# Met waits between the products of the output in 31 tiles of a fused Mamba and local-attention kernel

## The chip, the cores and the metric

The kernel runs on one core of one Trainium2 chip. The metric is device time in microseconds (us) of one execution. A core has a matrix engine (PE, which executes matmuls and, on a track called PEld, weight loads), a vector engine (DVE), an activation engine (ACT), a general engine (POOL) and an engine that issues DMAs (SP). Each has a sequencer of its own that walks through that engine's instructions in program order; engines meet only through semaphores, which count finished stages. A wait for a semaphore is an instruction of the waiting engine.

## The reference

The input is 4 sequences of 1024 tokens with 128 features, in float32. The reference normalises it, runs a bidirectional Mamba layer, and then six transformer layers. One transformer layer is, shortened:

```python
def attn_layer(x, Wqkv, qs, ksc, Wo):          # 16 heads of 64, window 32
    q, k, v = split(x @ Wqkv)                  # q, k: l2norm, scale, rotary
    out = local_attention(q, k, v)             # each window sees itself and the one before
    return out @ Wo
def ffn_layer(x, g, bln, W1, b1, W2, b2):
    a, gate = split(layernorm(x) * g + bln) @ W1 + b1
    return a * gelu(gate) @ W2 + b2
for i in range(6):
    x = attn_layer(shift_tokens(x), ...) + x
    x = ffn_layer(shift_tokens(x), ...) + x
```

The change touches `out @ Wo` of the attention, in the kernel a product of the mixed values with folded weights.

## The kernel before, in words

The Mamba layer fills the first 1,070 us or so. Then come the six layers, worked through in 192 tiles of 128 tokens (32 per layer, numbered 0 to 191 through all layers); four tiles are a chunk. For a tile PE does: `project0` and `project1` (L1043, queries and keys), four `head_turn` transposes (L1054), `score` (L1078 and L1093), `row_turn` (L1065), `mix` (L1105), `output` (L1116). Per chunk there are the feed-forward stages (L1141, L1154) and two means (L1123, L1129).

The order of these stages on PE is a table, `PE_ORDER`, one round per chunk, with stages of neighbouring chunks interleaved. The other engines have tables like it. So the work ahead of a tile's score or output depends on the tile's place in its chunk, its number modulo 4, and hardly on anything else; the text calls it place 0 to 3.

`after(engine, (stage, k))` (L900) puts in a wait until stage `k` is done. Several waits ahead of one matmul become separate wait instructions of PE, two waits in each, and the last wait rides on the matmul's weight load.

The number of an instruction in PE's program is counted as follows. A product of float32 operands is four instructions (two weight loads and two matmuls), a transpose or a product of rounded or bfloat16 operands two, a separate wait one. The score of a tile is 64 float32 products of 32 to 64 columns, 256 instructions, after two bfloat16 products (L1078). The trace shows each float32 product as two matmuls, so a score has 128 matmuls, and an output, 16 products, has 32. In this text "pair" means one weight load with its matmul; a score has 128 pairs.

Of the kernel before, what the change touches and what calls it, by code (L numbers as in the profile page):

```python
# [651 lines left out]
DEPTH, HEADS, HEAD_DIM, WINDOW = 6, 16, 64, 32  # L652
PAIRS = HEADS // 2
INNER = HEADS * HEAD_DIM
HIDDEN = int(DIM * 4 * 2 / 3)
HIDDEN_PARTS = [(0, P), (P, P), (2 * P, HIDDEN - 2 * P)]
QK_SCALE = 8.0
TILES = TOKENS // P
# [21 lines left out]
def head_at(place):  # L680

    return place % PAIRS * 2 + place // PAIRS
# [145 lines left out]
def transformer(nc, ctx, consts, xa, xb, resid, kept, kept_stored, hbm, out, stored):  # L828

    def sb(name, shape, dt=F32):  # L830
        return ctx.enter_context(nc.sbuf_tensor(name, shape, dt))
# [9 lines left out]
    w_vo = sb("w_vo", [P, 2, HEADS, P])  # L841
    w1_parts = sb("w1_parts", [P, 2, 2 * HIDDEN], F32R)
    w2 = sb("w2", [P, 2, 3, P])
# [29 lines left out]
    work = sb("work_ff", [P, BANK])  # L873
    hidden = [sb(f"hidden{k}", [m, BANK]) for k, (_, m) in enumerate(HIDDEN_PARTS)]
    ff_parts = sb("ff_parts", [P, 2, BANK], F32R)
# [5 lines left out]
    score_ps = ps[:, S:S + 2, :].rearrange("p b (h k) -> p (b h) k", k=2 * WINDOW)  # L881
    w1_raw = w_stage[:, 0:2 * HIDDEN]
    w_v, w_o = vo_stage[:, 0], vo_stage[:, 1]
# [16 lines left out]
    def after(eng, *producers):  # L900
        for name, k in producers:
            eng.wait_ge(done[name], k + 1)
# [6 lines left out]
    def indexed(name, f, n):  # L909
        return {f"{name}{i}": f(i) for i in range(n)}  # L910
# [12 lines left out]
    def place(tile):  # L923
        return tile // TILES, tile % TILES, tile % 2

    with nc.Block() as block:
# [63 lines left out]
        def _(pe):  # L990
# [11 lines left out]
            def turn_free(name, k, i=0):  # L1002
                last = TURNS[name, k, i][1]
                if last and last[0] == "ff_output":
                    ff_added(pe, CHUNKS + last[1])
                elif last and last[0] in ("fold0", "fold1"):
                    pe.wait_ge(vo_copied, 4 * last[1] + 2 * int(last[0] == "fold1") + last[2] + 1)
                elif last and last[0] == "mix":
                    after(pe, (f"copy_mixed{last[2]}", last[1]))
                elif last and last[0] == "in_variance":  # L1010
                    pe.wait_ge(done["in_rstd"], 2 * last[1] + 1)
                elif last:
                    after(pe, (TURN_READERS[last[0]], last[1]))
                return turn_bank(name, k, i)
# [94 lines left out]
            def output(tile):  # L1109
                l, t, odd = place(tile)  # L1110
                after(pe, *[(f"copy_mixed{w}", tile) for w in range(WINDOWS)])
                if t == 0:
                    pe.wait_ge(vo_copied, 4 * l + 4)
                bank = turn_free("output", tile)
                for place_h in range(HEADS):
                    last = pe.matmul(bank[:, 0:P], w_vo[:, l % 2, head_at(place_h), :], mixed[:, odd, place_h, :],  # L1116
                                     start=place_h == 0, stop=place_h == HEADS - 1)
                last.then_inc(done["output"], 1)

            def mean(chunk):  # L1120
# [10 lines left out]
            def hidden_part(name, first):  # L1131
                def part(k):
                    lo, m = HIDDEN_PARTS[k]

                    def stage(chunk):
                        after(pe, ("rest_high", chunk))
                        if chunk % CHUNKS == 0:
                            pe.wait_ge(w1_low, chunk // CHUNKS + 1)
                        bank = turn_free(f"{name}{k}", chunk)
                        for i, (wpart, xpart) in enumerate([(0, 0), (1, 0), (0, 1)]):  # L1140
                            last = pe.matmul(bank[0:m], w1_parts[:, wpart, first + lo:first + lo + m],  # L1141
                                             ff_parts[:, xpart, :], start=i == 0, stop=i == 2)
                        last.then_inc(done[f"{name}{k}"], 1)
                    return stage
                return part

            def ff_output(chunk):
# [4 lines left out]
                bank = turn_free("ff_output", chunk)  # L1152
                for k, (lo, m) in enumerate(HIDDEN_PARTS):
                    last = pe.matmul(bank, w2[0:m, l % 2, k, :], hidden[k][:, :], start=k == 0, stop=k == 2)  # L1154
                last.then_inc(done["ff_output"], 1)

            stages = {"in_centre": in_centre, "in_variance": in_variance, **indexed("fold", fold, 2), **indexed("project", project, 2), **indexed("head_turn", head_turn, 4),
                      "row_turn": row_turn, "score": score, "mix": mix,
                      "output": output, "mean": mean, "variance": variance,
                      **indexed("gate", hidden_part("gate", HIDDEN), 3), **indexed("value", hidden_part("value", 0), 3),  # L1160
                      "ff_output": ff_output}
# [4 lines left out]
        def _(act):  # L1166
# [120 lines left out]
            def gelu(k):  # L1287
                m = HIDDEN_PARTS[k][1]

                def stage(chunk):  # L1290
                    l = chunk // CHUNKS
                    if chunk % CHUNKS == 0:
                        act.wait_ge(w2_loaded, 32 * l + 32)
                    after(act, (f"gate{k}", chunk))
                    if chunk:
                        after(act, ("ff_output", chunk - 1))
                    act.activation(hidden[k][:, :], turn_bank(f"gate{k}", chunk)[0:m], ACT.Gelu,
                                   bias=lp[0:m, l % 2, GATE_B + k:GATE_B + k + 1]).then_inc(done[f"gelu{k}"], 1)
                return stage
# [26 lines left out]
        def _(dve):  # L1326
# [106 lines left out]
            def product(k):  # L1433
                m = HIDDEN_PARTS[k][1]

                def stage(chunk):
                    after(dve, (f"value{k}", chunk), (f"gelu{k}", chunk))
                    dve.scalar_tensor_tensor(out=hidden[k][:, :], in0=turn_bank(f"value{k}", chunk)[0:m],
                                             scalar=lp[0:m, chunk // CHUNKS % 2, A_B + k:A_B + k + 1],
                                             in1=hidden[k][:, :], op0=ALU.add, op1=ALU.mult).then_inc(done[f"product{k}"], 1)  # L1440
                return stage
# [188 lines left out]
def host_layout(inputs):  # L1630
# [11 lines left out]
    lp[:, :, LN_G], lp[:, :, LN_B], lp[:, :, OUT_B] = a["L0_ffn_ln_g"], a["L0_ffn_ln_b"], a["L0_ffn_b2"]  # L1642
    for k, (lo, m) in enumerate(HIDDEN_PARTS):
        w2[:, :m, k] = a["L0_ffn_W2"][:, lo:lo + m]
        lp[:, :m, A_B + k] = a["L0_ffn_b1"][:, lo:lo + m]
        lp[:, :m, GATE_B + k] = a["L0_ffn_b1"][:, HIDDEN + lo:HIDDEN + lo + m]
    return {
# [35 lines left out]
```

## Time and profile before

| | us |
|---|---|
| median of 2 runs | 3917.53 |
| the two runs | 3914.40, 3920.66 |
| span of the profiled execution, first to last instruction | 3921.5 |
| PE busy in that span | 3707.5 (95%) |
| POOL busy | 3241.5 (83%) |
| DVE busy | 3319.6 (85%) |
| ACT busy | 2915.4 (74%) |

A time of its own, beside its span, is not given for the profiled execution. Its span lies 4.0 us (0.1%) above the median of the runs. Busy shares of PE count a matmul until its modelled end, so successive matmuls overlap; the spacing of their starts is what a product costs. The rows that matter stand in a section below.

### The profile page before, as it was taken

The numbers are of one execution on the slowest core, as the hardware profiler recorded it, in microseconds if no ns is written. First come the engines' busy times: TensorE is split into PE (matmuls) and PEld (weight loads), VectorE is DVE, ScalarE is ACT, GpSimd is POOL, SyncE is SP. The second block draws the span as 40 slices with busy tenths as digits, with TensorE's granted clock in tenths as the row PEclk, the third lists the DMA queues.
The fourth block names the chain that finished last, engine by engine and source line by source line (L and its number), as shares of the span: only waits on it lengthen the run. The fifth ranks groups of instructions, "written<-read, shape, count | busy, mean of one in ns | idle before, by whom it ended". The sixth has DMA issues, their size and how long they took to land.

```text
span 3921.5 us, 110568 instructions
## 1 busy us (share of the span) xinstructions
PE 3707.5 (95%) x43392; PEld 2518.5 (64%) x43392; DVE 3319.6 (85%) x3407; ACT 2915.4 (74%) x6890; POOL 3241.5 (83%) x2370
## 2 busy tenths in 40 slices
PE   7889989988789999999999999999999999999997
PEld 2333333333377777777777777777767777777775
DVE  4999999999688888888888887888878888788885
ACT  7555445553388887888888887888878888888885
POOL 3888888888698888888888888888888888888883
PEclk8999998998899999999999999999999999999999
DMA  1221222212100000000000000000000000000001
GB/s 68 73 76 70 76 71 75 76 71 83 50 16 2 16 3 2 17 2 16 3 6 13 2 16 2 6 13 3 16 2 6 13 2 16 2 6 2 2 3 44
DMA packets 31567, 102.12 MB, mean 26 GB/s; under 512 B 4676, under 2 KB 6600, under 8 KB 30928
## 3 DMA queue, kind: packets, MB, share of 16 engines
q1 hardware_dynamic: 31056, 95.05, 7.0%
q8 instruction: 352, 5.77, 0.6%
q14 instruction: 159, 1.30, 0.1%
HBM read 90.32 MB, written 4.72 MB: 24 GB/s over the span
## 4 chain that ended last, share of the span: by engine, by line
PE 68%; issue 2%; ACT 2%; DVE 0%; POOL 0%; POOLq 0%; ACTq 0%; DVEq 0%
PE ps L1116 17%; PE ps L1043 13%; PE ps L1105 9%; PE ps L1054 8%; PE ps L1093 7%; PE ps L1141 5%; PE ps L1154 3%; PE ps L1078 2%; PE ps L1065 1%; PE ps L1123 1%; PE ps L1129 1%; ACT prob L1246 0%; PE ps L1023 0%; ACT mixed L1255 0%; ACT w_qk L1175 0%
## 5 line engine op out<-in xcount | busy, mean ns | idle before, releaser
L1521 POOL TENSOR_TENSOR resid<-resid,sq 128x1024 f32<-128x1024 f32 x384 | 910.8, 2377 | 3.4 <-DVE sq L1376 2.9
L626 POOL TENSOR_TENSOR read<-state,c_row 128x1024 f32<-128x1024 f32 x256 | 719.8, 2831 | 153.9 <-DVE state L588 84.9
L1543 POOL TENSOR_TENSOR resid<-resid,rnorm 128x1024 f32<-128x1024 f32 x384 | 725.0, 1904 | 18.1 <-POOL rnorm L1535 0.4
L1116 PE MATMUL ps<-mixed,w_vo 128*128 128x128 f32 x6144 | 720.7, 276 | 3.0 <-ACT mixed L1255 2.8
L1116 PEld LDWEIGHTS ps<-mixed,w_vo 128*128 128x128 f32 x6144 | 711.5, 193 | 12.9 <-issue 4.6
L1043 PE MATMUL ps<-w_qk,xs_parts 128*128 128x512 f32 x2304 | 634.6, 411 | 35.4 <-issue 18.1
L1246 ACT ACTIVATE prob<-ps,stat 128x64 f32<-128x64 f32 x3072 | 653.5, 385 | 0.7 <-DVE stat L1396 0.5
L1376 DVE TENSOR_TENSOR sq<-ps,rope_l 128x1024 f32<-128x1024 f32 x384 | 462.4, 1204 | 101.5 <-ACT sq L1208 101.2
L393 PE MATMUL mamba_ps<-read,ident 128*128 128x512 f32 x1024 | 509.6, 638 | 15.4 <-POOL read L626 15.4
L1389 DVE TENSOR_TENSOR resid<-ps,rope_l 128x1024 f32<-128x1024 f32 x384 | 464.3, 1209 | 66.9 <-ACT sq L1208 59.7
L1043 PEld LDWEIGHTS ps<-w_qk,xs_parts 128*128 128x128 f32 x2304 | 412.4, 191 | 148.6 <-issue 73.8
L1550 POOL TENSOR_TENSOR prob<-prob,stat 128x1024 f32<-128x1024 f32 x192 | 366.1, 1907 | 165.3 <-DVE stat L1407 165.3
L1208 ACT ACTIVATE sq<-ps 128x1024 f32<-128x1024 f32 x384 | 395.7, 1030 | 141.3 <-PE ps L1043 111.8
L1255 ACT COPY mixed<-ps 128x512 f32<-128x512 f32 x768 | 399.5, 602 | 111.8 <-PE ps L1105 111.7
L522 ACT ACTIVATE decay<-dt,neg_a 128x1024 f32<-128x1024 f32 x256 | 280.4, 1143 | 268.1 <-DVE state L588 212.6
L1353 DVE TENSOR_REDUCE ssq<-sq 128x16 f32<-128x1024 f32 x384 | 465.7, 1213 | 6.1 <-ACT sq L1208 1.7
L1054 PE MATMUL ps<-ident,resid 128*128 128x128 f32 x3072 | 414.4, 275 | 13.7 <-ACT w_vo L1190 13.1
L588 DVE TENSOR_TENSOR_SCAN state<-decay,mamba_ps 128x1024 f32<-128x1024 f32 x176 | 396.3, 2274 | 3.7
L1054 PEld LDWEIGHTS ps<-ident,resid 128*128 128x128 f32 x3072 | 351.3, 141 | 74.6 <-issue 60.8
L1105 PE MATMUL ps<-prob_t,rows 32*128 32x512 f32 x3072 | 385.2, 613 | 4.1 <-DVE xb L1424 1.6
L393 PEld LDWEIGHTS mamba_ps<-read,ident 128*128 128x128 f32 x1024 | 196.9, 202 | 283.5 <-issue 247.1
L1230 ACT COPY q_t<-ps 128x512 f32<-128x512 f32 x384 | 230.9, 602 | 127.0 <-PE ps L1054 125.0
(138 smaller groups left out, 5676.8 us busy)
## 6 DMA issues: line engine op xcount, KB each, us to landing
c_row<-c_rows SPq DMA_DIRECT2D x128, 512.0 KB, 3.6
w_stage<-w_qk_hbm SPq DMA_DIRECT2D x12, 512.0 KB, 4.7
vo_stage<-w_v_hbm SPq DMA_DIRECT2D x6, 512.0 KB, 3.7
vo_stage<-w_o_hbm SPq DMA_DIRECT2D x6, 512.0 KB, 4.6
xn<-x_hbm SPq DMA_DIRECT2D x4, 512.0 KB, 6.6
kept<-resid SPq DMA_DIRECT2D x8, 256.0 KB, 4.4
resid<-kept SPq DMA_DIRECT2D x8, 256.0 KB, 4.0
out_hbm<-resid SPq DMA_DIRECT2D x8, 256.0 KB, 2.0
```

The source lines that it names most:

```text
L393: last = pe.matmul(y_ps[h][:, c, :], ident[:, :], read[:, h, g % 2, cols(c)], start=False, stop=n == LAST)
L626: pool.tensor_tensor(read[:, h, g % 2, :], state[:, h, g % 2, :], c_row[:, g % C_AHEAD, :], ALU.mult).then_inc(done[f"rd{h}"], 1)
L1043: last = pe.matmul(ps[:, A + c, :], xs_parts[:, odd, xpart, :], w_qk[:, wpart, cols], start=k == 0, stop=k == 2)
L1054: last = pe.transpose(bank[:, j * P:(j + 1) * P], qk[:, tile % 2, col:col + P], ident[:, :])
L1105: last = pe.matmul(banks[w], rows[rows_w, tile % 2, own, :], prob_t[rows_w, tile % 2, :, own, :], start=own == 0, stop=own == 1)
L1116: last = pe.matmul(bank[:, 0:P], w_vo[:, l % 2, head_at(place_h), :], mixed[:, odd, place_h, :], start=place_h == 0, stop=place_h == HEADS ...
L1246: last = act.activation(prob[:, tile % 2, place_h, :], score_ps[:, place_h, :], ACT.Exp, bias=stat[:, tile % 2, 0, place_h:place_h + 1])
L1353: dve.tensor_reduce(ssq[:, tile % 2, part * HEADS:(part + 1) * HEADS, 0], sq[:, 0, :].rearrange("p (h d) -> p h d", d=HEAD_DIM), AX_X, ALU ...
L1376: dve.tensor_tensor(sq[:, 1 + part, :].rearrange("p (h s d) -> p h s d", s=2, d=HEAD_DIM // 2), swapped, table(part, 1, tile).rearrange("p ...
L1389: dve.tensor_tensor(qk[:, tile % 2, part * INNER:(part + 1) * INNER].rearrange("p (h d) -> p h d", d=HEAD_DIM), heads_ps.rearrange("p (h d ...
L1521: pool.tensor_tensor(qk[:, tile % 2, cols], qk[:, tile % 2, cols], sq[:, 1 + part, :], ALU.add).then_inc(done[f"rotated{part}"], 1)
L1543: pool.tensor_tensor(heads, heads, norms, ALU.mult).then_inc(done[f"normed{part}"], 1)
```

## The change

In 31 of the 192 tiles, waits for `copy_mixed0` of the same tile are put ahead of the products 2 to 16 of `output`. The first product has waited for that very stage already, so each of the new waits is met when PE's sequencer comes to it. A table gives the number of added wait instructions per tile, from 16 to 60; the code spreads them over the 15 places between the products, the larger shares first (60 is four at each place, 35 is three at five places and two at ten). Of the `2 * spaced` waits at a place the last rides on the next product's weight load, and the others make `spaced` separate wait instructions (two waits in each, one in the odd one). In all, 1,363 instructions are added to PE's program; the order of the work on every engine is the same, and so are all products.

```diff
+FETCH_PADS = {0: 35, 3: 35, 15: 58, 16: 58, 17: 34, 21: 34, 26: 41, 39: 60, 40: 60, 41: 28, 53: 60, 54: 55, 60: 60, 61: 42, 
+    73: 18, 85: 59, 86: 56, 92: 59, 93: 43, 105: 17, 117: 59, 118: 56, 124: 59, 125: 43, 137: 17, 149: 49, 
+    154: 39, 167: 16, 175: 60, 176: 16, 184: 37}
@@ output(tile)
                 for place_h in range(HEADS):
                     last = pe.matmul(bank[:, 0:P], w_vo[:, l % 2, head_at(place_h), :], mixed[:, odd, place_h, :],
                                      start=place_h == 0, stop=place_h == HEADS - 1)
+                    spaced = (FETCH_PADS.get(tile, 0) + HEADS - 2 - place_h) // (HEADS - 1) if place_h < HEADS - 1 else 0
+                    for _ in range(2 * spaced):
+                        after(pe, ("copy_mixed0", tile))
                 last.then_inc(done["output"], 1)
```

PE's program about the output of tile 60 (place 0; 60 added waits), with the semaphores that each matmul and the wait instructions ahead of it wait for; L1043 is a projection, L1129 a variance, L1065 the row turns, L1116 the output. Before:

```order
L1043 MATMUL ps<-w_qk,xs_parts 128x512 [waits sines1,cosines1,rest]
L1043 MATMUL ps<-w_qk,xs_parts 128x512 x5
L1129 MATMUL ps<-work_ff,ones_mean 128x512 [waits copy_mixed0,square]
L1065 MATMUL ps<-ident,xa 128x128 [waits copy_mixed1,x_ready,x_low]
L1116 MATMUL ps<-mixed,w_vo 128x128 [waits copy_mixed3,copy_mixed2,copy_mixed1,copy_mixed0]
L1116 MATMUL ps<-mixed,w_vo 128x128 x15
L1054 MATMUL ps<-ident,resid 128x128 [waits copy_mixed3,normed0]
```

And now (the lines below the table of pads have moved by three, those below the output by six):

```order
L1046 MATMUL ps<-w_qk,xs_parts 128x512 [waits sines1,cosines1,rest]
L1046 MATMUL ps<-w_qk,xs_parts 128x512 x5
L1135 MATMUL ps<-work_ff,ones_mean 128x512 [waits copy_mixed0,square]
L1068 MATMUL ps<-ident,xa 128x128 [waits copy_mixed1,x_ready,x_low]
L1119 MATMUL ps<-mixed,w_vo 128x128 [waits copy_mixed3,copy_mixed2,copy_mixed1,copy_mixed0]
L1119 MATMUL ps<-mixed,w_vo 128x128 [waits copy_mixed0] x15
L1057 MATMUL ps<-ident,resid 128x128 [waits copy_mixed3,normed0]
```

Nothing has changed places; 15 of the 16 products now have waits ahead of them (four instructions each here, which the row shows once).

The same about the output of tile 85 (place 1; 59 added waits), where L1141 is a gate product and L1054 a head turn. Before:

```order
L1054 MATMUL ps<-ident,resid 128x128 [waits copy_mixed3,normed1]
L1054 MATMUL ps<-ident,resid 128x128 x3
L1141 MATMUL ps<-ff_parts,w_parts 128x512 [waits copy_heads0,rest_high]
L1141 MATMUL ps<-ff_parts,w_parts 128x512 x2
L1116 MATMUL ps<-mixed,w_vo 128x128 [waits copy_mixed3,copy_mixed2,copy_rows,copy_mixed1,copy_mixed0]
L1116 MATMUL ps<-mixed,w_vo 128x128 x15
L1054 MATMUL ps<-ident,resid 128x128 [waits x_ready,x_low,normed1]
```

And now:

```order
L1057 MATMUL ps<-ident,resid 128x128 [waits copy_mixed3,normed1]
L1057 MATMUL ps<-ident,resid 128x128 x3
L1147 MATMUL ps<-ff_parts,w_parts 128x512 [waits copy_heads0,rest_high]
L1147 MATMUL ps<-ff_parts,w_parts 128x512 x2
L1119 MATMUL ps<-mixed,w_vo 128x128 [waits copy_mixed3,copy_mixed2,copy_rows,copy_mixed1,copy_mixed0]
L1119 MATMUL ps<-mixed,w_vo 128x128 [waits copy_mixed0] x15
L1057 MATMUL ps<-ident,resid 128x128 [waits x_ready,x_low,normed1]
```

Here too only the 15 later products have gained waits, and every instruction of PE behind them has a higher number in the program.

## Rows read from the trace of the kernel before

**Rows 1.** The page, part 1: busy us, share of the span, instructions of each engine.

```profile
PE 3707.5 (95%) x43392; PEld 2518.5 (64%) x43392; DVE 3319.6 (85%) x3407; ACT 2915.4 (74%) x6890; POOL 3241.5 (83%) x2370
```

**Rows 2.** Windows view, layers: us, busy us per engine (PE, PEld, DVE, ACT, POOL), clock, DMA.

```profile
1500.00:3850.00 2350.00, 2318.10 (x34556) 1791.23 (x34555) 1980.77 (x2321) 1970.49 (x5230) 2024.62 (x1723) 1.00 0.02 7
```

**Rows 3.** Waits of PE, 1500 to 3850 us: total us, times, longest.

```profile
PE ps L1043 <- issue: 14.4, 5, 3.6
PE ps L1093 <- issue: 2.7, 9, 0.5
```

**Rows 4.** The page, part 3: DMA queue, packets, MB, share of 16 engines.

```profile
q8 instruction: 352, 5.77, 0.6%
```

**Rows 5.** Source view of L902, PE's separate waits: duration ns min/median/max, first and last start.

```profile
L902 PEldq EVENT_SEMAPHORE  x3111: 51/51/3933, 1041.4 to 3911.3; - x195
```

**Rows 6.** Timeline of PE, scores of tiles 4, 33 and 185: start, us, matmuls, idle before.

```profile
1123.36 1.31 PE L1093 MATMUL ps<-k_t,q_t 64*32 64x64 f32 x109
1125.04 0.41 PE L1093 MATMUL ps<-k_t,q_t 64*32 64x64 f32 x19 [0.36 <-issue]
...
1551.47 1.48 PE L1093 MATMUL ps<-k_t,q_t 64*32 64x64 f32 x128
...
3781.47 1.47 PE L1093 MATMUL ps<-k_t,q_t 64*32 64x64 f32 x126
3783.39 0.27 PE L1093 MATMUL ps<-k_t,q_t 64*32 64x64 f32 x2 [0.46 <-issue]
```

**Rows 7.** DMA view, packets that started from 1122.3 to 1122.4 us: packets, MB, share.

```profile
q8 instruction: 1, 0.02, 77.5%
```

**Rows 8.** Timeline of PE, scores of tiles 96 and 124.

```profile
2479.51 1.46 PE L1093 MATMUL ps<-k_t,q_t 64*32 64x32 f32 x128
...
2883.38 1.20 PE L1093 MATMUL ps<-k_t,q_t 64*32 64x64 f32 x100
2884.91 0.45 PE L1093 MATMUL ps<-k_t,q_t 64*32 64x64 f32 x28 [0.33 <-issue]
```

**Rows 9.** Source view of L902, windows of 0.01 us from 2047.41, 2047.52, 2047.62.

```profile
L902 PEldq EVENT_SEMAPHORE  x1: 51/51/51, 2047.4 to 2047.4; - x1
L902 PEldq EVENT_SEMAPHORE  x1: 51/51/51, 2047.5 to 2047.5; - x1
L902 PEldq EVENT_SEMAPHORE  x1: 51/51/51, 2047.6 to 2047.6; - x1
```

**Rows 10.** Source views, last waits ahead of an output and its loads: tiles 72, 85, 54, 175.

```profile
L902 PEldq EVENT_SEMAPHORE  x3: 51/51/369, 2156.7 to 2157.2; - x3
L1116 PEld LDWEIGHTS ps<-mixed,w_vo x32: 190/192/192, 2157.4 to 2160.9; 128*128 128x128 f32 x32
L902 PEldq EVENT_SEMAPHORE  x2: 51/51/51, 2342.0 to 2342.1; - x2
L1116 PEld LDWEIGHTS ps<-mixed,w_vo x32: 189/192/192, 2344.2 to 2347.8; 128*128 128x128 f32 x32
L902 PEldq EVENT_SEMAPHORE  x3: 51/51/51, 1887.0 to 1887.5; - x3
L1116 PEld LDWEIGHTS ps<-mixed,w_vo x32: 190/192/192, 1888.1 to 1891.6; 128*128 128x128 f32 x32
L902 PEldq EVENT_SEMAPHORE  x4: 51/51/51, 3668.8 to 3669.2; - x4
L1116 PEld LDWEIGHTS ps<-mixed,w_vo x32: 188/192/192, 3670.6 to 3674.1; 128*128 128x128 f32 x32
```

**Rows 11.** Timeline of PE, the output of tile 72.

```profile
2157.51 3.74 PE L1116 MATMUL ps<-mixed,w_vo 128*128 128x128 f32 x32
```

**Rows 12.** Windows view, PE idle, just after, and a half-busy stretch; columns as in rows 2.

```profile
1494.26:1497.85 3.59, 0.00 (x1) 0.03 (x1) 2.20 (x4) 1.28 (x5) 3.59 (x3) 1.00 0.00 0
1498.50:1501.90 3.40, 3.40 (x10) 2.49 (x9) 0.39 (x1) 1.02 (x1) 3.02 (x7) 0.50 0.01 2
1027.47:1030.88 3.41, 2.01 (x5) 0.35 (x3) 2.79 (x5) 3.38 (x6) 2.92 (x4) 1.00 1.01 363
```

## The prediction

> **What bounds the kernel now.** The page's busy line comes first: PE is busy for 95% of the span, no other engine for more than 85% [rows 1]. The window over the layers sharpens it: of 2350 us PE is busy for 2318, at a granted clock of 1.00 (the level of 2.4 GHz) [rows 2]. So in the layers nearly every microsecond that PE loses lengthens the run, and the other engines have 15% of slack to follow. PE's waits there are few: 14.4 us in five pieces of up to 3.6 us at the start of a layer (L1043), which the change does not touch, and 2.7 us put down to "issue" in the scores (L1093) [rows 3]. "Issue" means that PE waited for nothing on record, and that is where the change aims.
>
> The timeline shows what it is. An undisturbed score of 128 pairs stands as one row of 1.48 us, as in tile 33 [rows 6]. In tile 4 it breaks after 109 pairs, and goes on 1.68 us after its start; in tile 185 it breaks after 126 [rows 6]. From tile 2 on, 25 scores are lengthened like this, tile 4 the first and tile 185 the last, by up to 0.83 us and by 9.0 us together. (The 2.7 us above is less, because a gap within a matmul's modelled length of 0.2 us doesn't count as idle.) The place of the break follows the program: counted from zero, the first matmul behind the largest gap has number 196 or 197 modulo 256 in 24 of the 25. The DMA queue that carries instructions moved 352 packets of 16 KB [rows 4], and PE's program is 43,392 matmuls, as many weight loads [rows 1] and over 3,111 waits [rows 5], 256 instructions per packet. Ahead of tile 4's break such a packet started between 1122.3 and 1122.4 us [rows 7], and the score went on at 1125.04 [rows 6], some 2.7 us later. So I read it thus: PE's instructions come in blocks of 256, a block is asked for when the sequencer passes an earlier block's end, and where the next 256 instructions take less time than the delivery, PE stands. Only a score is dense enough: its 256 instructions pass in 1.26 us (1.48 less the last matmul's 0.22), 5 ns each.
>
> **What it gains.** The added waits shift every later block end. A break needs the block's end late in the score: all 25 lie behind pair 91 of 128, since an earlier end puts the block's beginning far back in slower work. Counted in the programs, 53 of the scores from tile 2 have a block end at pairs 91 to 126 before, and 41 after. Of these 41, 15 stand at place 0 of their chunk, at pairs 91 to 104. Before, 12 scores of place 0 lay there and five were lengthened, by 1.2 us together, 0.10 each; tile 96 went through and tile 124 lost 0.5 [rows 8]. Fifteen times 0.10 is 1.5 us. Four stand at places 1 and 3, for which I take 0.05 each, between nothing and the 0.10. The other 22 are at place 2, where no score had such an end before. There the block begins in a row of 20 transposes, which PE takes over 2 us for, and the sequencer waits between them for other engines; so I take nothing, with 22 times 0.17 (9.0 over 53, the mean of all places), 3.7 us, as the upper bound. The stalls fall from 9.0 to 1.7 us: **a gain of 7.3 us**, with 3.6 and 9.0 as bounds.
>
> A page of the Trainium skill speaks against this term: "Runtime: NRT & Kernel Launch", section "Instruction fetch mechanics", says that the crossing of a 16 KiB block is mostly hidden, since the sequencer dispatches more slowly than the blocks are filled. By it nothing could be gained, and the sum would be the cost below alone. Tile 4's break [rows 6] contradicts it in the scores.
>
> **What it costs.** 1,363 wait instructions are new, all met when they are reached. In the trace such a wait lasts 51 ns [rows 5], but neighbouring waits do not start 51 ns apart: a run of three ahead of a mix starts at 2047.41, 2047.52 and 2047.62 us [rows 9], 0.105 each, and in the whole trace no two start closer than that. I take 0.106 us of the sequencer per wait. The lower bound is the 0.051.
>
> What hides them is PE's own pace. An output's 32 weight loads start from 2157.4 to 2160.9 us in tile 72 [rows 10], 0.112 us apart, so that the stage takes 3.57 us (the timeline's 3.74 [rows 11] has the last matmul's length in it), and a place between two products is worth 0.223 us. The sequencer needs 4 x 5 ns for a product and 0.106 per wait: 0.13, 0.23, 0.34 and 0.44 us for one to four waits. One or two are covered; three or four are not, and PE runs dry unless the sequencer entered the stage ahead. How far ahead depends on the place, and is read as the time from the end of the last wait before the output to its first load: 0.13 us at place 0 (tile 72), 2.1 at place 1 (tile 85), 0.6 at place 2 (tile 54), 1.3 at place 3 (tile 175) [rows 10]. With p waits the sequencer takes 0.32 + 0.106 p, PE 3.57, so the stage grows by 0.106 p - 3.25 - lead, where that is positive:
>
> - Place 0, eight tiles (0, 16, 40, 60, 92, 124, 176, 184): 0.3, 2.8, 3.0, 3.0, 2.9, 2.9, 0 and 0.5, together 15.4 us.
> - Place 1, 13 tiles: only 53, 85 and 117 have over 50 waits: 1.0, 0.9, 0.9, together 2.8 us.
> - Place 2, five tiles (26, 54, 86, 118, 154): 0.5, 2.0, 2.1, 2.1, 0.3, together 7.0 us.
> - Place 3, five tiles: 15, 39 and 175 have over 43: 1.6, 1.8, 1.8, together 5.2 us.
>
> That is 30.4 us. Behind the waits stand, on PE, the next head turns and projections, and for the output's end waits DVE's sum; both move with PE, so nothing else is added, and nothing in a window where PE is 98.6% busy takes it back. By the lower bound, 0.051 us, four waits and a product take 0.224 us, PE's own pace, and the cost is nothing.
>
> A figure of the skill lies between the bounds: "Advanced Engine Details and Errata", section "Miscellaneous Facts", gives 50 to 100 ns for a sequencer's reading of a semaphore. By its lower end the estimate is a cost of nothing and a sum of 3910; no run here shows a wait repeated faster than 0.105 us.
>
> **The sum.** On the profiled execution, 3921.5 + 30.4 - 7.3 = 3944.6 us of span. The median of the runs lies 4.0 below that span; 3917.5 + 23.1 gives 3940.6, **3941 us** (+0.6%).
>
> **Rivals.**
> 1. *The waits stay hidden; not slower.* If a met wait takes the sequencer 0.051 us when no profiler records it, four per place just fit into 0.223 us, and only the gain is left: 3917.5 - 7.3 = 3910 us. For it speaks the recorded length [rows 5], and that a profiled sequencer may be slowed; against it the spacing [rows 9]. It decides at 0.051; already at 0.08 a place with four waits takes 0.34 us, and place 0 alone loses 7 us. Chance 0.22.
> 2. *The block ends move, but the stalls come back elsewhere* (at place 2, or because a sequencer that has lost its lead crosses the block's beginning later). Then the gain shrinks to nothing: 3917.5 + 30.4 = 3948 us. Chance 0.12.
> 3. *The clock falls in the thinned outputs.* After a pause of PE of 3.59 us the granted clock read 0.50 (1.2 GHz) for 3.40 us [rows 12]. A padded output leaves PE without new work for half of its time, in pieces of 0.2 us. A stretch of the Mamba part with PE at 2.01 of 3.41 us kept 1.00 [rows 12], so I think it holds. If it fell for 3.4 us behind each of the 14 outputs with 55 or more waits, at half pace, that would be 14 x 1.7 = 24 us more: 3965 us. Chance 0.08.
>
> My forecast keeps 0.58; between 3925 and 3953 us by its bounds (a lead that is larger in part, 0.111 us per wait, a gain of 3.6 to 9.0). The range reaches down to rival 1 and up over rival 2: **3909 to 3953 us**, which leaves out rival 3 and some edges. A measurement of this kernel tells about 2% (78 us) from no change, and none of these cases reaches that: faster 0.01, same 0.97, slower 0.02, the last for a clock that falls more often than in rival 3.
>
> **What would show it.** Right: in the profile after, the output of tile 60 or 40 takes some 6.5 us instead of 3.57, in bursts of two products' matmuls 0.44 us apart, and the outputs of tiles 61, 93 and 125 take 3.57 as before; added waits start 0.105 us apart; most of the 25 scores that broke before pass in 1.48 us, and the remaining breaks stand at place 0, at pairs 91 to 104. Wrong: outputs of 3.7 us with four waits a place (rival 1), scores at place 2 broken at pairs 97 to 104 (rival 2), or a granted clock under 1.00 behind padded outputs (rival 3).

## The result, and the profile after

The changed kernel takes 3966.92 us (3965.96 and 3967.88) against 3917.53 before: a ratio of 1.0112, with a 95% interval from 1.0095 to 1.0128, so 37 to 50 us more. The forecast was 3941, its range ended at 3953. The profiled execution has a span of 3964.2 us, 42.7 more than before.

The page first, answering [rows 1, 4]: PE's busy time and PE's instruction packets.

```profile
PE 3744.2 (94%) x43392; PEld 2530.4 (64%) x43392; DVE 3320.6 (84%) x3407; ACT 2917.1 (74%) x6890; POOL 3242.5 (82%) x2370
...
q8 instruction: 358, 5.87, 0.6%
```

The other engines do what they did, to within 2 us. PE's busy time grew by 36.7 us with the same matmuls: the profile models a matmul's end and draws it out where the next one comes late. Six packets more are 1,536 instructions, room for the 1,363 that were added. The next fence is the windows view of the layers, answering [rows 2], and of the output of tile 60 alone (us, busy us of PE, PEld, DVE, ACT, POOL, clock, DMA share, GB/s).

```profile
1500.00:3893.00 2393.00, 2353.97 (x34698) 1805.47 (x34699) 1982.40 (x2324) 1974.06 (x5234) 2030.60 (x1727) 1.00 0.02 7
...
1998.80:2006.10 7.30, 7.00 (x36) 4.84 (x35) 2.35 (x2) 4.42 (x18) 4.75 (x3) 1.00 0.01 2
```

PE still bounds the layers, and the clock stays at 1.00 (2.4 GHz), in the padded output too: rival 3 did not come. Then the source view of the separate waits, answering [rows 5], in the whole run and over the added waits of tile 60 (1998.66 to 2005.63 us), and the output's loads there, answering [rows 10].

```profile
L905 PEldq EVENT_SEMAPHORE  x4474: 51/51/3932, 1042.5 to 3953.2; - x195
...
L905 PEldq EVENT_SEMAPHORE  x60: 51/51/51, 1998.7 to 2005.6; - x60
...
L1119 PEld LDWEIGHTS ps<-mixed,w_vo x32: 186/189/192, 1998.7 to 2005.8; 128*128 128x128 f32 x32
```

4,474 less 3,111 are the 1,363 new waits. The 60 of tile 60 start from 1998.67 to 2005.57 us, all met. In the 31 outputs, 833 of the spacings between added waits are 0.105 or 0.106 us (with a product between, most are 0.125 or 0.126). The first starts 0.05 us ahead of the output's first load, and the last wait in front of the output ended 0.13 ahead of it: the lead that the prediction gave to place 0.

The timeline shows both halves of the result. First two outputs, tile 60 with 60 waits (place 0) and tile 61 with 42 (place 1), answering [rows 11]:

```profile
1998.83 0.72 PE L1119 MATMUL ps<-mixed,w_vo 128*128 128x128 f32 x4
1999.72 6.42 PE L1119 MATMUL ps<-mixed,w_vo 128*128 128x128 f32 x28 [0.17 <-issue]
...
2017.40 3.73 PE L1119 MATMUL ps<-mixed,w_vo 128*128 128x128 f32 x32
```

Tile 60 takes 7.31 us instead of 3.74, tile 61 what it took before. The idle 0.17 at 1999.72 is a pause of the sequencer, 32 instructions behind a block's end. Now the scores of tiles 4 and 185, which broke before [rows 6], of tiles 40 and 74, and what follows the scores of tiles 103 and 135:

```profile
1122.74 1.48 PE L1096 MATMUL ps<-k_t,q_t 64*32 64x64 f32 x128
...
3819.78 1.48 PE L1096 MATMUL ps<-k_t,q_t 64*32 64x64 f32 x128
...
1655.88 1.20 PE L1096 MATMUL ps<-k_t,q_t 64*32 64x32 f32 x103
1657.44 0.43 PE L1096 MATMUL ps<-k_t,q_t 64*32 64x64 f32 x25 [0.36 <-issue]
...
2169.68 1.68 PE L1096 MATMUL ps<-k_t,q_t 64*32 64x64 f32 x128
...
2605.29 1.48 PE L1096 MATMUL ps<-k_t,q_t 64*32 64x64 f32 x128
...
2607.20 0.27 PE L1068 MATMUL ps<-ident,xa 128*128 128x128 f32 x1
2608.23 0.27 PE L1068 MATMUL ps<-ident,xa 128*128 128x128 f32 x1 [0.76 <-issue]
...
3084.51 1.48 PE L1096 MATMUL ps<-k_t,q_t 64*32 64x64 f32 x128
...
3087.57 1.64 PE L1046 MATMUL ps<-w_qk,xs_parts 128*128 128x512 f32 x6 [0.77 <-issue]
```

Tiles 4 and 185 pass in 1.48 us, tile 40 breaks after 103 pairs, and tile 74 (place 2) is drawn out to 1.68. The scores of tiles 103 and 135 pass, but PE stands a few matmuls behind them, in the second row turn and ahead of the projection, some 1.0 us each over the usual spacing. The waits view from 1500 to 3893 us, answering [rows 3], has these lines on "issue" (engine, line, waited for: us, times, longest):

```profile
PE ps L1046 <- issue: 18.0, 6, 3.6
...
PE ps L1057 <- issue: 2.7, 6, 0.6
PE ps L1068 <- issue: 1.2, 2, 0.8
PE ps L1096 <- issue: 1.0, 3, 0.4
PE ps L1108 <- issue: 1.0, 3, 0.4
```

"Issue" fell from 2.7 to 1.0 us in the scores, and appeared in the head turns, row turns and mixes (L1057, L1068, L1108), where there had been none. The 18.0 us of L1046 are the starts of the layers, one of which falls inside the window only now, and the 0.77 ahead of tile 135's projection. In full, each block end against the usual spacing at its place (the median over both traces; excesses over 0.06 us counted):

| | stalls in scores, us | 0 to 17 matmuls behind, us | span, us |
|---|---|---|---|
| before | 9.0 (25) | 2.5 (8) | 3921.5 |
| after | 3.3 (11) | 11.9 (17) | 3964.2 |

So the account of the 42.7 us is: 40.2 in the padded outputs, 3.7 more at block ends, 1.7 less in the outputs without pads, 0.5 elsewhere. The 1.7 come from nothing that the prediction weighed: 1.6 of them stand in the last output, tile 191's, where the granted clock read 0.50 (1.2 GHz) for 3.4 us before and 1.00 now. (It read 0.50 there in the spread and the first clear kernel too, and 1.00 in the struck and the second clear one; why is not shown.) The windows view of that output, before and after:

```profile
3887.90:3891.20 3.30, 3.30 (x18) 3.30 (x17) 0.00 (x0) 0.00 (x0) 0.00 (x0) 0.50 0.00 0
...
3928.30:3931.80 3.50, 3.50 (x31) 3.50 (x32) 0.00 (x0) 0.00 (x0) 0.00 (x0) 1.00 0.00 0
```

### The profile page after: what moved, and what is told of

It reads as the page before. It is cut to its first block, busy times and chain, and to the rows that moved or that the text cites. A ratio compares the mean times of both kernels' runs of the same rounds, so it can differ in the third digit from the quotient of the medians.

```text
span 3964.2 us, 111931 instructions
## 1 busy us (share of the span) xinstructions
PE 3744.2 (94%) x43392; PEld 2530.4 (64%) x43392; DVE 3320.6 (84%) x3407; ACT 2917.1 (74%) x6890; POOL 3242.5 (82%) x2370
## 4 chain that ended last, share of the span: by engine, by line
PE 69%; issue 2%; ACT 1%; DVE 0%; POOL 0%; POOLq 0%; DVEq 0%; ACTq 0%
PE ps L1119 18%; PE ps L1046 13%; PE ps L1108 9%; PE ps L1057 8%; PE ps L1096 7%; PE ps L1147 5%; PE ps L1160 3%; PE ps L1081 2%; PE ps L1068 1%; PE ps L1129 1%; PE ps L1135 1%; ACT prob L1252 0%; PE ps L1026 0%; ACT mixed L1261 0%; ACT w_vo L1196 0%
## 5 line engine op out<-in xcount | busy, mean ns | idle before, releaser
L1119 PE MATMUL ps<-mixed,w_vo 128*128 128x128 f32 x6144 | 756.9, 278 | 5.4 <-ACT mixed L1261 2.8
L1119 PEld LDWEIGHTS ps<-mixed,w_vo 128*128 128x128 f32 x6144 | 724.7, 192 | 38.3 <-issue 14.1
L1046 PE MATMUL ps<-w_qk,xs_parts 128*128 128x512 f32 x2304 | 636.1, 412 | 33.9 <-issue 18.0
L1046 PEld LDWEIGHTS ps<-w_qk,xs_parts 128*128 128x128 f32 x2304 | 413.6, 191 | 149.8 <-issue 71.5
L1057 PE MATMUL ps<-ident,resid 128*128 128x128 f32 x3072 | 415.1, 275 | 16.2 <-ACT w_vo L1196 13.1
L1057 PEld LDWEIGHTS ps<-ident,resid 128*128 128x128 f32 x3072 | 351.4, 141 | 77.0 <-issue 62.9
L1108 PE MATMUL ps<-prob_t,rows 32*128 32x512 f32 x3072 | 388.4, 613 | 6.0 <-DVE xb L1430 1.6
```

The source lines that it names most:

```text
L1046: last = pe.matmul(ps[:, A + c, :], xs_parts[:, odd, xpart, :], w_qk[:, wpart, cols], start=k == 0, stop=k == 2)
L1057: last = pe.transpose(bank[:, j * P:(j + 1) * P], qk[:, tile % 2, col:col + P], ident[:, :])
L1108: last = pe.matmul(banks[w], rows[rows_w, tile % 2, own, :], prob_t[rows_w, tile % 2, :, own, :], start=own == 0, stop=own == 1)
```

## Experiments

Ratios are to the kernel before on the same chip. "Stalls" are counted as in the table above.

**Spread.** The waits of a tile's output are spread over the projections, head turns, gate and value products, mixes, outputs and feed-forward outputs between two scores. The score of tile k + 3 follows the output of tile k, so the keys are three higher. The cut shows two of the places at which `pad` is called.

```diff
-FETCH_PADS = {0: 35, 3: 35, 15: 58, 16: 58, 17: 34, 21: 34, 26: 41, 39: 60, 40: 60, 41: 28, 53: 60, 54: 55, 60: 60, 61: 42, 
+GAP_PADS = {3: 35, 6: 35, 18: 58, 19: 58, 20: 34, 24: 34, 29: 41, 42: 60, 43: 60, 44: 28, 56: 60, 57: 55, 63: 60, 64: 42, 76: 18,
...
+    def pad(pe, name, k, place, met):
+        for _ in range(2 * PADS.get((name, k, place), 0)):
+            after(pe, met)
...
+                            pad(pe, f"project{part}", tile, 3 * c + k, ("rest", tile))
...
+                    pad(pe, "output", tile, place_h, ("copy_mixed0", tile))
```

> The same 1,363 waits as in the changed kernel, but spread over all stages between two scores, mostly one or two to a place, so that every score still begins at the same program number as in the changed kernel. Theory (the loss is the density of waits in 19 outputs, +40.2 us in the profile; the block ends, moved from late in the scores to right behind them, cost 3.7 more than before): the 40 go, the stalls stay at about 15 us, some 12 of them behind the scores; 3917.5 + 3.7 and up to 2 for places with two waits, 3919 to 3924 us. Rival A (the loss comes from the number of waits, or of blocks fetched, wherever they stand): about 3960 to 3967 us. Rival B (the loss comes from where the block ends fall): also 3960 or more.

Measured: ratio 1.0030 (1.0019 to 1.0040), span 3937.3 us. The output of tile 60 and the score of tile 103, timeline:

```profile
1987.59 3.91 PE L1149 MATMUL ps<-mixed,w_vo 128*128 128x128 f32 x32
...
2583.19 1.48 PE L1124 MATMUL ps<-k_t,q_t 64*32 64x64 f32 x128
...
2586.12 0.27 PE L1096 MATMUL ps<-ident,xa 128*128 128x128 f32 x1 [0.76 <-issue]
```

All outputs together are 0.7 us longer than before: the 40 us were the waits' density, not their number, and rivals A and B, with 3960 us or more, fell. With the same program number at every score, the stall behind tile 103 is the same 0.76, and stalls behind the scores come to 13.6 us, in them to 6.5. By the ratio that is 3929 us, 5 more than the theory's upper end: stalls within the scores came to 6.5 and not 3.3. The largest new one is tile 150's, here and in the changed kernel:

```profile
3272.78 1.28 PE L1124 MATMUL ps<-k_t,q_t 64*32 64x64 f32 x104
3275.71 0.43 PE L1124 MATMUL ps<-k_t,q_t 64*32 64x64 f32 x24 [1.65 <-issue]
...
3301.15 1.48 PE L1096 MATMUL ps<-k_t,q_t 64*32 64x64 f32 x128
```

The block that ends there holds the same instructions in both kernels, and begins with the same 20 transposes (at 3270.18 us here, at 3298.55 there). But its packet started at 3273.08 us here, 2.9 behind the first of them, and at 3298.45 there, 0.1 ahead of it. The cause of that difference is not known.

**Clear.** The changed code with another table: 80 outputs, 2 to 15 waits each, 820 in all.

```diff
-FETCH_PADS = {0: 35, 3: 35, 15: 58, 16: 58, 17: 34, 21: 34, 26: 41, 39: 60, 40: 60, 41: 28, 53: 60, 54: 55, 60: 60, 61: 42, 
...
+FETCH_PADS = {8: 8, 12: 6, 16: 6, 19: 7, 20: 15, 21: 15, 22: 13, 23: 15, 24: 15, 25: 15, 26: 15, 27: 15, 31: 6, 35: 5, 39: 6, 43: 6,
...
```

> The changed kernel's code with another table: 820 waits in 80 outputs, at most 15 to an output (one to a place), chosen so that block ends keep clear of the stretch from pair 92 of a score to 13 matmuls behind it. Stalls at block ends were 11.6 us in the profile before and are 4.4 here by the table of both traces, and waits at one to a place are covered. Theory: 3917.5 - 7 = 3910 us (3906 to 3912). Rival A (number of waits counts): 820 of 1,363 waits, 0.6 x 49 = +30, 3947 us. Rival B (the stalls at block ends are an artefact of the profiler, or are made up later): 3917 us.

Measured: 1.0022 (1.0010 to 1.0034), span 3931.3. That is 3926 us, where the theory had 3906 to 3912, rival A 3947 and rival B 3917: none of them holds. Outputs are 0.2 us shorter in sum, but stalls are 19.5 us, all within scores. The table did not keep the block ends out: 49 scores have one at pair 92 or later, 29 of them stalled, and most of those at positions where an end had passed in the two traces that the table was made from, or within a few pairs of one (at place 0 after 116 pairs, where 115 and 117 had passed; at place 3 after 100, where two of three had). The score of tile 30, timeline and then the instruction packets that started from 1508.9 to 1509.0 us (packets, MB, share):

```profile
1504.16 1.09 PE L1060 MATMUL ps<-ident,resid 128*128 128x128 f32 x8
1506.56 1.55 PE L1060 MATMUL ps<-ident,resid 128*128 128x128 f32 x12 [1.31 <-ACT w_vo L1199]
...
1508.37 1.30 PE L1099 MATMUL ps<-k_t,q_t 64*32 64x64 f32 x106
1511.29 0.42 PE L1099 MATMUL ps<-k_t,q_t 64*32 64x64 f32 x22 [1.62 <-issue]
```

```profile
q8 instruction: 1, 0.02, 57.4%
```

The block that ends at pair 106 began at 1503.9 to 1504.5 us, with the second four of these transposes. Where nothing holds the sequencer a packet starts about 1.0 us after that, but here the sequencer was held by a wait for ACT until 1506.5, 10 instructions into the block, and none started before 1508.94. PE then went on 2.35 us after the packet's start, within the 2.1 to 3.2 of nearly all stalls. So the position of a block end alone does not tell whether it stalls; a wait that holds the sequencer at the block's beginning counts too.

**Struck.** The opposite table: 94 outputs, 2 to 22 waits each, 1,360 in all.

```diff
+FETCH_PADS = {1: 15, 2: 15, 3: 15, 4: 15, 5: 22, 6: 22, 7: 22, 11: 8, 15: 6, 19: 7, 20: 15, 21: 15, 22: 21, 23: 22, 24: 22, 25: 22,
...
```

> The opposite table: 1,360 waits (the changed kernel has 1,363) in 94 outputs, at most 22 to an output (one or two to a place), chosen so that as many block ends as possible fall from late in a score to just behind it. By the table of both traces the stalls come to 49 us instead of 11.6. Theory: 3917.5 + 37 = 3955 us (3940 to 3962), with no output longer than 3.6 to 3.9 us in the profile. If the waits alone counted (rival A): 3966 us with outputs of 5 to 6 us. If stalls at block ends were an artefact (rival B): 3917 us.

Measured: 1.0119 (1.0100 to 1.0139), 39 to 54 us more: 3964 us by the ratio, 2 over the end of the theory's range, which the interval reaches down into. Rival A's outputs of 5 to 6 us did not come: the outputs are no longer than before (1.5 us shorter in sum, by the clock in tile 191's); the mixes behind the scores of place 2 are 49 us longer; stalls come to 46.1 us behind scores and 12.1 in them. The score of tile 78, timeline, and the packet that started from 2220.0 to 2220.1:

```profile
2219.46 1.48 PE L1100 MATMUL ps<-k_t,q_t 64*32 64x64 f32 x128
2220.96 1.13 PE L1112 MATMUL ps<-prob_t,rows 32*128 32x512 f32 x4
2222.75 1.56 PE L1112 MATMUL ps<-prob_t,rows 32*128 32x512 f32 x10 [0.66 <-issue]
```

```profile
q8 instruction: 1, 0.02, 77.1%
```

Here a block is 122 of the score's 128 pairs, three waits and the first four matmuls of the mix, 256 instructions that PE passes in little over the score's 1.3 us, and PE goes on 2.7 us after the packet's start. All four runs show the loss (3963 to 3978 us, the profiled one the shortest), so rival B fell for the times on record. Each of these times comes with a span and a granted clock, and the record does not say that one was taken with nothing recording, so whether recording adds to the stalls is not shown.

**Price.** 256 waits in each of four outputs.

```diff
+FETCH_PADS = {16: 256, 40: 256, 60: 256, 124: 256}
```

> 256 waits in each of four outputs at place 0 (tiles 16, 40, 60, 124), 17 or 18 to a place, none elsewhere: each output is one block longer, so every score outside begins at the same number modulo 256 as in the kernel before, and only the price of a wait is left. Theory (0.106 us per wait with or without a profile): each output grows by 256 x 0.106 + 0.32 - 3.57 - 0.13 = 23.8 us, and by some 0.5 for a pause at its block end and the latencies, together 97 us: 4015 us. Rival C (0.051 us when no profiler records): 9.6 each, 39 us: 3956 us unprofiled, 4015 profiled.

Measured: 1.0274 (1.0257 to 1.0291), 107 us more in time, and a span 107.5 us longer. That is 10 more than forecast, some 3 of it in the outputs and 7 behind them. Rival C's 3956 us came in none of the four runs (4029 to 4033); as with the struck kernel, the record does not say that one of them was taken with nothing recording. The output of tile 60, timeline of its places 7 and 8; the waits between two such places (source view); and the windows view before, in and behind it:

```profile
2052.67 0.77 PE L1117 MATMUL ps<-mixed,w_vo 128*128 128x128 f32 x2 [1.08 <-issue]
2054.52 0.76 PE L1117 MATMUL ps<-mixed,w_vo 128*128 128x128 f32 x2 [1.08 <-issue]
```

```profile
L903 PEldq EVENT_SEMAPHORE  x17: 51/51/51, 2052.6 to 2054.3; - x17
```

```profile
2041.40:2043.30 1.90, 0.38 (x2) 0.20 (x3) 0.97 (x1) 1.90 (x11) 1.82 (x2) 1.00 0.00 0
2043.30:2045.20 1.90, 0.47 (x3) 0.32 (x3) 0.00 (x0) 0.51 (x3) 0.92 (x1) 0.68 0.04 9
...
2048.90:2067.60 18.70, 7.67 (x20) 5.01 (x20) 0.00 (x0) 0.00 (x0) 0.00 (x0) 0.50 0.00 1
...
2069.00:2072.00 3.00, 3.00 (x12) 2.03 (x14) 2.41 (x3) 1.71 (x4) 1.23 (x1) 0.62 0.00 0
2072.00:2075.00 3.00, 3.00 (x139) 1.69 (x134) 2.27 (x3) 2.96 (x6) 3.00 (x3) 1.00 0.00 0
```

A place of 17 waits takes 1.85 us, 0.109 each with the product and the pause in it. Each output grew by 24.9 to 25.1 us (formula: 23.8), and the stages behind it by 1.4 to 2.5: the granted clock read 1.00 (2.4 GHz) in the first 3.9 us of an output that kept PE busy for a quarter of the time, 0.68 in the next 1.9, and then 0.50 (1.2 GHz) to its end at 2067.65; from 2072 it read 1.00 again.

**Clear, second try.** The same code; 113 outputs, 4 to 15 waits each, 1,317 in all, one to a place.

```diff
+FETCH_PADS = {1: 4, 6: 15, 7: 15, 8: 15, 9: 10, 13: 6, 17: 6, 18: 4, 19: 15, 20: 15, 21: 15, 22: 15, 23: 7, 24: 15, 25: 15, 26: 15,
...
```

> A second try at keeping block ends clear, with the positions that five traces (before, changed, and the first three experiments) showed to pass or to break: 1,317 waits in 113 outputs, at most 15 to an output (one to a place). Theory (where the block's beginning lets the sequencer through at once and its end lies outside the crowded stretch, nothing stands; waits at one to a place are free): stalls at block ends 4 to 8 us in the profile instead of 11.6, so 3917 - 5 = 3912 us (3908 to 3918). Rival A (each wait costs something wherever it stands, by the second run's 10 us for 820): +16, 3933 us. Rival D (stalls come back at other positions whatever table is chosen, as in the second run): 20 us of stalls, 3926 us.

Measured: 1.0032 (1.0022 to 1.0042), span 3934.1. The theory failed. By the time, 3930 us, rivals A (3933) and D (3926) are about as near; the trace speaks for D: 20.2 us of stalls, all in 39 scores, and outputs no longer than before (1.3 us shorter in sum, by the clock in tile 191's). The scores of tiles 148 (one of 24 like it at place 0) and 154 (one of five at place 2):

```profile
3247.68 1.30 PE L1101 MATMUL ps<-k_t,q_t 64*32 64x64 f32 x106
3249.27 0.42 PE L1101 MATMUL ps<-k_t,q_t 64*32 64x64 f32 x22 [0.29 <-issue]
...
3336.21 1.43 PE L1101 MATMUL ps<-k_t,q_t 64*32 64x64 f32 x122
3339.00 0.31 PE L1101 MATMUL ps<-k_t,q_t 64*32 64x64 f32 x6 [1.36 <-issue]
```

At place 0 an end at pair 106 had passed in the kernel before (tile 64) and at pair 107 (tile 112), and stalls here at 24 of 29 scores, 0.2 to 0.6 us each. So the changed kernel and these two have 15 to 20 us of stalls where the kernel before has 11.5, and no version was found that beats the kernel before.

**Crossing.** 60 waits in eight outputs at place 0, with covered waits ahead of them that set where a block ends.

```diff
+FETCH_PADS = {11: 8, 12: 15, 13: 15, 14: 15, 15: 15, 16: 60, 39: 1, 40: 60, 55: 4, 56: 15, 57: 15, 58: 15, 59: 15, 60: 60, 91: 13,
...
```

> 60 waits (four to a place) in each of eight outputs at place 0, and covered waits at one to a place in the outputs ahead of them, which set where the block ends fall: in tiles 16, 60, 124 and 172 a block ends some 24 instructions behind the output's start, in tiles 40, 92, 156 and 188 it ends 70 instructions ahead of the output, and none within it. Forecast by the prediction's formula for all eight: 60 x 0.106 - 3.25 - 0.13 = 3.0 us longer than 3.46 (first to last product's start). Theory (the missing part of the cost is the sequencer's pause 30 to 50 instructions behind a block's end): tiles 16, 60, 124 and 172 grow by 3.4 to 3.6 us as in the changed kernel, tiles 40, 92, 156 and 188 by 3.0 to 3.2. Rival E (the missing part is a constant of any long run of waits): all eight grow by 3.4 to 3.6.

Measured (one run, 3981.54 us, span 3979.7): tiles 16, 60, 124 and 172, with a block end inside, grow by 3.62, 3.63, 3.63 and 3.61 us; tiles 40 and 156, without, by 3.57; tile 92, without, where the sequencer came 0.6 us early, by 2.79. Tile 188 is left out, since the granted clock read 0.50 at its start. Timeline of tiles 40 and 60:

```profile
1697.68 7.30 PE L1120 MATMUL ps<-mixed,w_vo 128*128 128x128 f32 x32
...
2000.19 1.71 PE L1120 MATMUL ps<-mixed,w_vo 128*128 128x128 f32 x8
2002.06 5.49 PE L1120 MATMUL ps<-mixed,w_vo 128*128 128x128 f32 x24 [0.17 <-issue]
```

By these numbers alone a block's end would be worth 0.06 us, and rival E would hold. But the tiles do not compare like for like. In the four, the last wait in front of the output ended 0.13 us ahead of the first load, as in the kernel before; in tiles 40 and 156 it ended 0.03 ahead, and the first product started 0.04 and not 0.11 behind that load, so that 0.18 us more of the sequencer's way fell into the stage. Against that, the pauses in the run of waits sum to 0.42 to 0.44 us in the four and to 0.20 in the two: a pause of 0.16 to 0.19 stands once behind the block's end (the 0.17 at 2002.06). So a block's end costs some 0.2 us, and neither the theory nor rival E holds alone. Of tile 40's 0.58 us over the formula, 0.18 is the missing lead, 0.20 are four pauses of 0.03 to 0.09 in the run of waits, 25 instructions apart, and the other 0.20 is the end: from the last added wait's start to the last product 0.29 us pass, 0.13 in the formula, and the stage of before is 3.46 from first to last start, not 3.57. The run's other 31 us are stalls (32.2 in all) and their like: the covered waits had shifted the scores by chance.

## Why the prediction was wrong

- **The bound** held. Every microsecond that PE lost came through to the span.
- **The reading of the stalls** as late instruction blocks held. In seven of the traces (all but that of the price) PE stalled at 242 of 2,027 block ends; at 229 of them it went on 2.1 to 3.2 us after the packet's start, and of the 1,785 that it passed without a stall it reached none sooner than 2.2 us after the packet's start, and 20 sooner than 2.6. The rule of the Trainium skill that was weighed there, "Runtime: NRT & Kernel Launch", section "Instruction fetch mechanics" (a crossing is mostly hidden), agrees with these 1,785 and not with the 242. Those bunch where PE passes a block fast: half of them within 3.3 us, against a median of 9 us at the ends that did not stall.
- **The gain failed**, at the sentence "A break needs the block's end late in the score". It was drawn from the 25 breaks within scores, and the count of 53 and 41 stopped at pair 126. What counts is how much of the 256 instructions is a score: a block that ends a few matmuls behind it is nearly all score (243 of its 256 instructions in tile 103). The trace of before had eight such stalls, 2.5 us, that the prediction did not look for. The scores alone gave 5.7 us (9.0 to 3.3), inside the bounds of 3.6 to 9.0; place 0 kept 2.2 and not 1.5, place 2 had 0.7 and not nothing. But 49 ends now lie within 14 matmuls behind a score, where 24 had; counted as in the table, 17 stalled there and lost 11.9. The net is 3.7 lost, not 7.3 gained. The spread kernel, with the same program numbers at the scores and the waits elsewhere, has these stalls again, and the struck one makes 46 us of them.
- **The cost** had its mechanism right: 0.105 us between waits; bursts 0.44 us apart at four waits; 107 us for the price kernel's 1,024; the tiles forecast as covered (61, 93, 125, 17, 21, 41) as long as before, though tile 149, covered by the formula too, grew by 0.29; the spread kernel frees the outputs. The size was wrong, 40.2 us and not 30.4, by some 0.3 to 0.6 in each of 19 exposed outputs. The failing term is the sequencer's account of a stage, 0.32 + 0.106 p: it knew no pauses in a long run of waits and no latency at its end. The largest: tiles 16, 40, 60, 92 and 124 grew by 3.37, 3.58, 3.57, 3.43 and 3.46 where it gave 2.8 to 3.0. Their leads were the 0.13 us assumed (0.12 to 0.14), their pauses sum to 0.37 to 0.40, of which 0.16 to 0.18 stand behind a block's end, and some 0.2 is the end of the stage.
- **Rivals.** The hidden waits (rival 1, 3910 us) are excluded by the result and the price, for times as they are measured here. Rival 2, stalls that come back elsewhere, is what happened, though mostly behind the scores, and with a net loss; in the scores of place 2 only 0.7 us came back. Rival 3's fall of the clock did not come at four waits a place; the price kernel shows it at 17.
- **The range** took the cost's upper bound from the waits alone (0.111 us each, a lead larger or smaller) and the gain's lower bound at 3.6, as if ends could not move to a worse place. With the measured terms the sum is 3917.5 + 40.2 - 1.7 + 3.7 + 0.5 = 3960 us, within the interval of 3955 to 3968. Of the 19.6 us between the span forecast (3944.6) and the one measured (3964.2), 11.0 are the gain that became a loss, 9.8 the cost, and -1.2 the rest. The remaining 7 us to the median of 3967 are no term of the trace: the profiled execution lay 4.0 us above the median before, and lies 2.7 below it now.

Open: what sets the moment at which the sequencer asks for a block. The packet started 1.0 us after the block's start where the sequencer ran on, and up to 6 us after where a wait held it within the first 60 instructions or so; a fixed instruction number does not fit all block ends, and in the spread kernel's tile 150 the packet came 3 us later than in the changed kernel behind the same instructions and waits. This is read from traces, no kernel varied it alone. Nor was the cause of the pauses in runs of waits looked for.

## What to carry to other kernels

Waits that are met are free only as long as the engine's own pace covers them, here two of 0.106 us for each 0.223 us of products, so padding belongs thinly spread over slow stages. Before shifting code to move block ends, list every stretch in which a whole block passes faster than the next can come, beyond the loop where the stalls were seen, and count the ends that fall into it afterwards. That count is no forecast by itself: ends at like positions stalled and passed here. A forecast of such a shift needs a bound for loss on the gain's side too, since another placement may be worse.

## What the hardware showed

- In the layers an instruction packet of PE took 0.88 to 1.57 us, and behind nearly all stalls PE went on 1.2 to 1.6 us after the packet's end.
- A run of met waits is interrupted each 19 (17 waits a place) or 25 instructions (four a place) by 0.03 to 0.09 us, and once behind a block's end by 0.14 to 0.19.
- With pairs of products 1.9 us apart, PE never idle for more than 1.6 us at a time, the granted clock did not stay at 1.00 (the price kernel, above); with pairs 0.44 us apart it did.
